# Mamba scan kernel: B rows and Gram sums moved to TensorE, bias operands folded into matmuls, split of quad 3 at 248

## What is computed

```python
# layer 0, per image, L = 4096 positions
u, z   = in_proj(group_norm(x))            # 96 -> 192 + 192 channels
u      = silu(causal_conv4(u) + conv_b)    # a bias per channel
dt, B, C = split(u @ x_proj.T, 6, 16, 16)
delta  = softplus(dt @ dt_proj.T + dt_bias)
h_t    = exp(delta_t * A) * h_(t-1) + delta_t * B_t * u_t   # 192 channels x 16 states
y      = (sum_n h_t[n] * C_t[n] + D * u) * silu(z)
x      = x + layernorm(y @ out_proj.T, eps=1e-5) * gamma + beta
# layer 1: t are tokens (4096 x 96)
t      = t + attention(layernorm(t, eps=1e-5))  # q (k' v): no softmax, so K'V folds into a 97 x 97 Gram matrix
t      = t + mlp(layernorm(t, eps=1e-5))        # 96 -> 384 -> 96, operands rounded to fp8, sums to fp16
```

## Time and profile before

| | |
|---|---|
| time of the runs | 2510.44 us median of 3 (2509.95 to 2512.78) |
| profiled execution, span from first to last instruction | 2508.8 us |
| busy share of the span | DVE 98%, POOL 96%, ACT 92%, PE 85% |
| mean granted clock of TensorE | 0.987 |

### The profile page before, as it was taken

The page is one execution under the profiler, slowest core; times in us unless marked ns, Lnnn a source line. Parts: engine busy times, 40 slices in busy tenths (PEclk is TensorE's granted clock), DMA queues, the critical chain, the costliest instruction groups (busy, mean ns, idle before and its releaser), DMA issues.

```text
span 2508.8 us, 35019 instructions
## 1 busy us (share of the span) xinstructions
PE 2142.1 (85%) x10314; PEld 826.0 (33%) x10314; DVE 2454.5 (98%) x2391; ACT 2314.7 (92%) x3960; POOL 2414.8 (96%) x655
## 2 busy tenths in 40 slices
PE   6788888888888888888888888888888888888878
PEld 3334434323323323323333323323323333333323
DVE  7999999999999999999999999999999999999986
ACT  5777777999999999999999999999999999999977
POOL 4999999999999999999999999999999999999991
PEclk8999999999999999999999999999999999999979
DMA  6555555556656656566566566566566565566542
GB/s 243 189 185 172 195 185 184 202 198 207 209 202 205 207 201 212 201 205 206 204 206 214 194 208 212 195 210 208 198 210 211 197 207 201 192 206 203 186 142 75
DMA packets 171388, 494.54 MB, mean 197 GB/s; under 512 B 23072, under 2 KB 44704, under 8 KB 154240
## 3 DMA queue, kind: packets, MB, share of 16 engines
q1 hardware_dynamic: 171200, 492.30, 57.9%
HBM read 400.33 MB, written 91.88 MB: 196 GB/s over the span
## 4 chain that ended last, share of the span: by engine, by line
POOL 40%; issue 40%; DVE 15%; PE 3%; ACT 1%; DMA 0%; POOLq 0%; DVEq 0%; SPq 0%; ACTq 0%
POOL R L676 20%; DVE R L1277 11%; POOL D L649 9%; POOL R L672 7%; POOL du L642 3%; DVE D L1261 2%; POOL D L658 2%; PE G L1568 1%; PE Y L1568 0%; DVE q L1357 0%; DVE dl L1287 0%; DVE G L1302 0%; DVE h L1471 0%; DVE h L1478 0%; PE Y L1645 0%
## 5 line engine op out<-in xcount | busy, mean ns | idle before, releaser
L1277 DVE TENSOR_TENSOR_SCAN R<-DA,R,D 128x512 f32<-128x512 f32 x1344 | 1630.2, 1263 | 1.0 <-ACT DA L840 1.0
L840 ACT ACTIVATE DA<-ds,kept_w 128x512 f32<-128x512 f32 x1536 | 1054.8, 688 | 139.9 <-DVE R L1277 127.1
L676 POOL TENSOR_TENSOR R<-R,Cs 128x2048 f32<-128x2048 f32 x255 | 970.9, 3819 | 4.0 <-DVE R L1277 2.6
L649 POOL TENSOR_TENSOR D<-us,Bs 128x2048 f32<-128x2048 f32 x193 | 736.9, 3818 | 8.8 <-DMA us<-lo_d 8.8
L672 POOL TENSOR_TENSOR R<-R,Cs 128x4096 f32<-128x4096 f32 x64 | 476.5, 7446 | 0.1
L1261 DVE TENSOR_TENSOR D<-us,PB 128x2048 f32<-128x2048 f32 x191 | 356.8, 1868 | 6.3 <-DMA us<-lo_d 6.3
L1645 PE MATMUL Y<-R,kept_w 128*32 128x512 f32 x2048 | 266.1, 615 | 13.9 <-POOL R L672 12.8
L1602 PE MATMUL G<-un,wcv 96*128 96x512 f32 x512 | 251.6, 614 | 29.5 <-ACT h L907 29.5
L1277 DVE TENSOR_TENSOR_SCAN R<-DA,D 128x512 f32<-128x512 f32 x192 | 221.7, 1204 | 2.1 <-ACT DA L840 2.1
L1605 PE MATMUL G<-un,wcv 96*64 96x256 f32 x1024 | 138.5, 392 | 60.1 <-ACT xq L888 58.9
L1568 PE MATMUL G<-st,kept_w 128*64 128x256 f32 (+1 forms) x384 | 108.9, 485 | 53.5 <-ACT st L802 53.5
(11 more groups left out here) (240 smaller groups left out, 3437.5 us busy)
## 6 DMA issues: line engine op xcount, KB each, us to landing
Bs<-bc_d SPq DMA_DIRECT2D x128, 512.0 KB, 5.6
us<-lo_d SPq DMA_DIRECT2D x64, 1024.0 KB, 6.3
ds<-lo_d SPq DMA_DIRECT2D x64, 1024.0 KB, 8.4
Cs<-bc_d SPq DMA_DIRECT2D x128, 512.0 KB, 4.7
us<-hi_d SPq DMA_DIRECT2D x64, 512.0 KB, 6.8
ds<-hi_d SPq DMA_DIRECT2D x64, 512.0 KB, 5.5
lo_d<-dl SPq DMA_DIRECT2D x64, 256.0 KB, 2.0
lo_d<-du SPq DMA_DIRECT2D x64, 256.0 KB, 2.0
```

Of the source, the lines that this page charges most:

```text
L649: nc.gpsimd.tensor_tensor(shaped(D[:, s % NDBU, :, :], s), low(us, s) if s in LOWS else high(us), of_states(Bs, s), ALU.mult).then_inc(don ...
L676: nc.gpsimd.tensor_tensor(shaped(R[:, s, :, 0:T], s), shaped(R[:, s, :, 1:S], s), of_states(Cs, s), ALU.mult).then_inc(hc_done.sem, 1)
L840: nc.scalar.activation(DA[j % NDA][:, :], ds[:, i, :], ACT.Exp, scale=A[:, j:j + 1]).then_inc(exp_done.sem, 1)
L1277: nc.vector.tensor_tensor_scan(R[:, s, q, 1:S], DA[j % NDA][:, :], D[:, s % NDBU, q, :], before, ALU.mult, ALU.add).then_inc(scanned.sem, 1)
```

## The change

Four parts, with the helper functions that carry them:

1. **Gram.** TensorE first multiplies G (SBUF) with an identity (`id97`) into G2, then adds the four token products; ScalarE copies the sum back to G (new `gram` on ScalarE, after decay(1, 2) and before `state_rows`). VectorE's add goes, save for the last two chunks.
2. **B rows.** `put_b` leaves ScalarE. TensorE makes PB from the state rows st with a selecting matrix of 32 rows (`bsel`): for quad 1 ahead of all else in an iteration, for quad 3 between `out_proj` and the centre matmuls, for the next chunk's quad 0 between `variance(g-1, 1)` and the conv. st gets two buffers.
3. **Biases.** A row of ones is added to un, sq, fsq and st, and conv_b, eps and dt_bias become a row of the weights; the activations lose their bias tensor. `state_rows` copies 64 rows in place of 128.
4. **Split.** `SPLIT = {3: 248}`: VectorE makes 16 columns more of each of the four blocks of quad 3, GpSimd 16 fewer.

```diff
-SPLIT = {3: 232}
+SPLIT = {3: 248}
...
+            sp_eng.dma_start(wcv[C:C + 1, 0, :], I["conv_b"]).then_inc(cb_in, 16)
...
-                    nc.scalar.activation(u[:, place(k) % 2, part(v)], src[v], ACT.Silu, bias=cb[:, v:v + 1])\
+                    nc.scalar.activation(u[:, place(k) % 2, part(v)], src[v], ACT.Silu)\
...
-                nc.scalar.activation(st[:, :], src[:, :], ACT.Identity, bias=one_row).then_inc(st_done.sem, 1)
+                nc.scalar.copy(st[0:64, k % 2, :], src[0:64, :]).then_inc(st_done.sem, 1)
...
-                nc.scalar.copy(PB[:, 0:n], Bs[:, h, w, 0:n]).then_inc(b_put.sem, steps_to(k, s))
...
-                nc.scalar.activation(rs[:, :], src[0:C, :], ACT.Ln, bias=epsn[0:C, :]).then_inc(post_ln.sem, 1)
+                nc.scalar.activation(rs[:, :], src[0:C, :], ACT.Ln).then_inc(post_ln.sem, 1)
...
+            def gram(k, src):
+                act.wait_ge(post_mm.sem, post_mm.at(k, 6))
+                if place(k) == 0 and there(k - CH):
+                    act.wait_ge(fold_mm.sem, fold_mm.at(k - CH, 1))
+                nc.scalar.copy(G[:, :], src[0:C + 1, 0:C + 1]).then_inc(gram_kept.sem, 1)
...
-                if there(g - 2):
-                    gram(g - 2, G2)
...
             def gram(k, o):
+                more = place(k) > 0 and k < LAST - 1
+                if more:
+                    pe.wait_ge(gram_kept.sem, gram_kept.at(k - 1))
+                    mm(o[0:C + 1, 0:C + 1], id97, G[:, :], start=True, stop=False)
...
+            def put_b(k, s):
+                if k == 0 and s == 1:
+                    return
+                if s == 3 and place(k + 3) == 0 and later(k + 3):
+                    pe.wait_ge(gn_act.sem, gn_act.at(k + 3, 4))
+                pe.wait_ge(st_done.sem, st_done.at(k))
+                pe.wait_ge(dbu_d.sem, dbu_d.at(k, BY_DVE[s] - steps_to(k, s)))
+                n = SPLIT.get(s, T)
+                one(PB[:, 0:n], bsel[:, BY_DVE[s] - 1, :], st[0:2 * STATE, k % 2, 0:n]).then_inc(b_put.sem, steps_to(k, s))
```

More of the change, by code:

```diff
@@ L777, in norm @@
                     act.wait_ge(front_mm.sem, front_mm.at(k - 1))
-                    nc.scalar.copy(un[:, 0:HALO], zero[0:C, 0:HALO])
-                nc.scalar.activation(un[:, lo:], un[:, lo:], ACT.Identity, bias=cgs[:, 1:2],
+                    nc.scalar.copy(un[0:C, 0:HALO], zero[0:C, 0:HALO])
+                nc.scalar.activation(un[0:C, lo:], un[0:C, lo:], ACT.Identity, bias=cgs[:, 1:2],
                                      scale=cgs[:, 0:1]).then_inc(normed.sem, 1)
@@ L871, in last_ln @@
                     act.wait_ge(post_dve.sem, post_dve.at(LAST - 1, 2))
-                nc.scalar.activation(rs[:, HALVES[h]], src[0:C, HALVES[h]], ACT.Ln, bias=epsn[0:C, :])\
+                nc.scalar.activation(rs[:, HALVES[h]], src[0:C, HALVES[h]], ACT.Ln)\
                     .then_inc(half_ln[h], 1)
@@ L897, in inv_ln_x2 @@
                 act.wait_ge(f_q8.sem, f_q8.at(m - 1))
-                nc.scalar.activation(frs[:, :], src[0:C, :], ACT.Ln, bias=epsn[0:C, :]).then_inc(f_ln.sem, 1)
+                nc.scalar.activation(frs[:, :], src[0:C, :], ACT.Ln).then_inc(f_ln.sem, 1)
             def inv_std_x2(m):
@@ L959, in iteration @@
                     decay(g, 1, 2)
+                if there(g - 2) and g - 2 < LAST - 1:
+                    gram(g - 2, G2)
                 if there(g + 1):
@@ L1087, in beginning @@
             def beginning():
-                nc.scalar.copy(un[:, 0:HALO], zero[0:C, 0:HALO])
+                nc.scalar.copy(un[0:C, 0:HALO], zero[0:C, 0:HALO])
                 act.wait_ge(x_in, 16)
                 act.wait_ge(gn_act.sem, gn_act.at(0))
-                nc.scalar.activation(un[:, HALO:], un[:, HALO:], ACT.Identity, bias=gsh[:, :],
+                nc.scalar.activation(un[0:C, HALO:], un[0:C, HALO:], ACT.Identity, bias=gsh[:, :],
                                      scale=gsc[:, :]).then_inc(normed.sem, 1)
@@ L1096, in beginning @@
                     act.wait_ge(front_mm.sem, front_mm.at(0, 1 + v))
-                    last = nc.scalar.activation(u[:, 0, part(v)], src[:, 0:T - H * v], ACT.Silu, bias=cb[:, v:v + 1])
+                    last = nc.scalar.activation(u[:, 0, part(v)], src[:, 0:T - H * v], ACT.Silu)
                     last.then_inc(silued.sem, 1)
@@ L1601, in conv @@
                     if v == 0:
[L1602 removed]
+                        last = mm(o[:, :], wcv[0:rows_of(t), t, 0:LOW], un[0:rows_of(t), t:t + T], start=(t == 0), stop=(t == TAPS - 1))
                         continue
                     for rows, cs in halves():
[L1605 removed]
+                        last = mm(o[rows, 0:H], wcv[0:rows_of(t), t, LOW:LOW + HIGH],
+                                  un[0:rows_of(t), t + cs.start:t + cs.stop],
                                   start=(t == 0), stop=(t == TAPS - 1))
@@ L1611, in z_proj @@
                 if v == 0:
-                    last = one(o[:, :], wz[:, 0:LOW], un[:, HALO:])
+                    last = one(o[:, :], wz[:, 0:LOW], un[0:C, HALO:])
                 else:
                     for rows, cs in halves():
-                        last = one(o[rows, to:to + H], wz[:, LOW:LOW + HIGH], un[:, HALO + cs.start:HALO + cs.stop])
+                        last = one(o[rows, to:to + H], wz[:, LOW:LOW + HIGH], un[0:C, HALO + cs.start:HALO + cs.stop])
                 last.then_inc(front_mm.sem, 1)
@@ L1630, in dt_proj @@
                 if v == 0:
-                    last = one(o[:, :], dtw[:, 0:LOW], st[:, :])
+                    last = one(o[:, :], dtw[0:65, 0:LOW], st[0:65, k % 2, :])
                 else:
                     for rows, cs in halves():
-                        last = one(o[rows, 0:H], dtw[:, LOW:LOW + HIGH], st[:, cs])
+                        last = one(o[rows, 0:H], dtw[0:65, LOW:LOW + HIGH], st[0:65, k % 2, cs])
                 last.then_inc(back_mm.sem, 1)
@@ L1714, in gram @@
                         pe.wait_ge(last_tokens, 1 + a // 2)
-                    last = mm(o[0:C + 1, 0:C + 1], tT[:, a, :], tT[:, a, :], start=(a == 0), stop=(a == T // 128 - 1))
+                    last = mm(o[0:C + 1, 0:C + 1], tT[:, a, :], tT[:, a, :], start=(a == 0 and not more),
+                              stop=(a == T // 128 - 1))
                 last.then_inc(post_mm.sem, 1)
+            def put_b(k, s):
[7 more added lines that the diff above has]
+                one(PB[:, 0:n], bsel[:, BY_DVE[s] - 1, :], st[0:2 * STATE, k % 2, 0:n]).then_inc(b_put.sem, steps_to(k, s))
             def fold(k, n, o):
@@ L1798, in iteration @@
                     pe.wait_ge(w_ready, 1)
+                if there(g):
+                    put_b(g, 1)
                 if there(g - 1):
@@ L2150 @@
         "skip": skip,
[L2151 removed]
+        "mask": (c[:, None] // hd == c[None, :] // hd) * hd ** -0.5,
     }
```

124 lines of the change are left out of this document (61 added, 63 removed).

## The result

The changed kernel takes 2533.55 us (median of 4 runs, 2531.08 to 2534.15), the kernel before 2510.39 beside it: a ratio of 1.0087, 95% interval 1.0073 to 1.0101. That is slower, as forecast, but by 23.2 us where 6.9 were forecast, and above the end of my range (2525). The profiled execution spans 2532.0 us against 2508.8, so it shows the whole difference: +23.15 us.

The account below looks back on a forecast made before the run. VectorE sets the pace, ScalarE and GpSimd close behind. First chunks of batches +3.0, plain chunks +4.9, first twelve chunks -1.0, the rest 0: +6.9 us on 2508.8, 2515.7, as a median 2517.3; range 2504 to 2525.

Parts of the forecast that it names:

- Steps 1 to 4: Plain chunk: state rows 0.39 us late behind Gram; TensorE 0.30 later; quad 3 adds 0.73; logarithm 0.36 later, `scale_out` 0.19.
- hole: TensorE's idle time ahead of `add_skip`: 1.18 us free, which the quad 1 matmul at 1.17 us just fits.
- The floor: Plain chunk: decay(2,1) ends later behind the state rows, so the scan needing it waits some 0.09 us.
- the 32-row tiles change nothing: Rival: no price for changing tile size, quad 3 matmul 0.42 us, plain chunks unchanged, 2510 to 2512 us; 25 in 100.
- the saving lands: Rival: neither floor nor `scale_out` is late, VectorE's saving gives -5 us or more, 2503 to 2505.5 us; 13 in 100.
- the plain chunk: 26 chunks without extra work in the whole pipeline: 0.19 us longer each through a later `scale_out`, 4.9 us together.
- the first chunk of a batch: Six chunks where VectorE already waited at `scale_out` and `variance` had no idle time ahead: 0.5 us longer each, 3.0 together.
- the 20 chunks taken as 0: Chunks with statistics, folds or set_batch: other work ahead of `scale_out` hides TensorE's delay; 0, between -0.1 and +0.19 us each.
- the whole -0.08: First 12 chunks: VectorE's net saving of 0.08 us a chunk (-0.15 for the add, +0.07 for the split) lands, -1.0 us.
- steps 1 to 3: State rows 0.39 us late behind Gram, TensorE 0.30 later, quad 3 matmul adding 0.73 ahead of the variance.
- the start: Before the first scan: one small DMA more on SP, taken as cancelling with shorter logarithms at the end, 0 us.
- The slack that the prediction worked out for `scale_out`: 0.40 us before `variance`, 0.19 before the logarithm, 0.09 of bias, 0.08 at `scale_out`: 0.76 in all.

Follow-up runs that it names:

- e1: The changed kernel with a 65-row selector for all three B-row matmuls, so their tile has the other matmuls' size: 2517.88 us, ratio 1.0021 to the kernel before.
- e2: The changed kernel with ScalarE's copy of G moved behind the state rows and decay(1,3): 2507.29 us, ratio 0.9977 to the kernel before.
- e9: The changed kernel with all three B rows back as ScalarE copies, Gram part, biases and split 248 kept: 2517.78 us, ratio 1.0024 to the kernel before.
- e7: The changed kernel with TensorE's quad 3 B-row matmul moved behind the two variances: 2863.05 us, ratio 1.1416 to the kernel before.
- e4: The changed kernel with the Gram part undone, VectorE adding to G again: 2514.19 us, ratio 1.0006 to the kernel before.
- e5: The changed kernel with the copy of G behind decay(1,3) and the quad 3 split back at 232: 2510.36 us, ratio 0.9996 to the kernel before.
- e6: The changed kernel with the copy of G behind decay(1,3) and the 65-row selector, split 248: 2504.61 us, ratio 0.9984 to the kernel before.
- e8: The changed kernel with Gram sum, B rows and split 232 put back, only the biases in matmul rows left: 2510.71 us, ratio 0.9998 to the kernel before.
- e10: The changed kernel with ScalarE's copy of G between the state rows and decay(1,3): 2507.71 us, ratio 0.9983 to the kernel before.
- e3: The changed kernel with quad 3's B row copied by ScalarE behind decay(2,1) instead of a TensorE matmul: 2526.66 us, ratio 1.0065 to the kernel before.
- e11: The changed kernel with copy of G behind decay(1,3), 65-row selector, and conv bias row's transfer behind the first weights': 2510.49 us, ratio 0.9992 to the kernel before.

## Why the prediction was wrong, by its own steps

**Right: what bounds the kernel, and the chain.** Steps 1 to 4 are in the rows almost as written. State rows +0.38 (forecast 0.39); TensorE +0.30 behind them (dt_proj at 11.45 instead of 11.16: 0.29); the quad 3 matmul 0.61 to the next start, 0.09 more at its entry and 0.08 on the matmul behind it, 0.78 (forecast 0.73); variance end +0.60 (0.55); logarithm +0.41 (0.36); `scale_out` +0.23 (0.19). The quad 1 matmul fits its hole: no wait appears at the gates that it could have held up in plain chunks. The floor, a scan waiting for decay(2,1), is there with 0.08 us (0.09), stays in e1 and goes when the copy moves. Of the rivals, "the 32-row tiles change nothing" is refuted by 0.36 us in e1, and "the saving lands" is true of e2, not of the change.

**Mis-sized: the plain chunk,** 0.25 for 0.19, 0.9 us over 26 chunks, and the first chunk of a batch, 0.53 for 0.5. The latter is near in part by luck: the forecast had all of it at `scale_out`, where VectorE waits for 0.31 us in chunk 16 (before 0.13), and missed 0.26 and 0.12 us of waits for decays ahead of two scans.

**Failed: the 20 chunks taken as 0.** This is the largest part of the miss, 8.15 of the 16.2 us between +6.9 and +23.1. The text said that with statistics, folds or set_batch an engine has work of its own ahead of `scale_out`, behind which TensorE's delay lies. It looked at one end of the chain, `scale_out`, and not at the new wait itself. In the statistics chunk the copy of G waits for a Gram group that stands behind the statistics' matmuls, and what it holds is not hidden: VectorE is later than before by 0.28 us at scan(1,3), 0.52 at scan(2,1), 0.68 at `scale_out`, 0.70 in the end. e9 (0.63 without any B row on TensorE) and e2 (-0.01 with the copy moved) show that nearly all of this is the copy's place. Over all 20 it was 8.15 us, of which 4.8 in the seven chunks of the statistics' place (4.5 in the six that have them), 1.9 in one second chunk (33) in which the clock fell for 3.4 us, and the rest mostly the plain chunk's 0.27 in the six second chunks.

**Failed: "the whole -0.08" in the first twelve,** -1.0, measured +4.7. 3.4 of this is chunk 1, where the clock was at its lower level for a stretch of 6.8 us that the execution of before did not have. Of the other kernels e7 had the same stretch (+3.1), e4, e5, e6, e8 and e10 had one of 3.4 us there (+1.0 to +1.8), and e1, e2, e3, e9 and e11 none (-0.4 to +1.05). That it makes the chunk longer is shown; that the change brings it on is not, since e2 and e10, which have the same matmuls, differ in it. What chunk 1 costs is the least sure part of the 23 us. Chunks 2 to 11 are +1.4 together. The prediction read from the earlier trace rows that of VectorE's own waits the one that recurs is `scale_out`'s. The same view of before has a larger one, for the second gate:

```profile
DVE yv L1298 <- PE Y L1649: 5.9, 9, 1.3
```

Eight of these nine waits lie in the first twelve chunks (0.31 to 0.46 us each in chunks 3 to 8). In the changed kernel they are gone in chunks 3 to 8, and waits at `scale_out` stand in their place, 0.27 us in chunks 2 to 7 and 0.55 in chunk 8, with 0.65 us ahead of scan(1,3) in the statistics chunk 5. With either cost of the chain away the same ten chunks come to -0.7 (e1) and -1.3 (e2), near what the prediction took. So steps 1 to 3 reach VectorE in them too, which the text had ruled out, since `spin` stands there in place of the centre matmuls.

**Open: the start,** +0.97 where 0 was taken; see e11.

**What the sum left out.** The prediction added terms along one chain with slack. The plain chunk is a table of the two costs, as the difference from before:

| | small tile for quad 3 | full tile |
|---|---|---|
| copy of G ahead of the state rows | +0.25 | +0.02 |
| copy of G behind decay(1,3) | -0.10 | -0.10 |

Either cost taken away frees VectorE almost wholly or wholly; both together give nothing more in this chunk. Removing the copy's place is worth 0.35 with the small tile and 0.12 with the full one; that 0.12 is the floor at scan(2,1) and little else. The slack that the prediction worked out for `scale_out` (0.76 us) fits: the change delays TensorE's matmuls up to the variance by 0.29 + 0.78 = 1.07 us, e1 by 0.29 + 0.42 = 0.71, e2 by 0.78 - 0.09 (its state rows end earlier) = 0.69, and only the first exceeds it. But the text did not ask what the order of one queue alone was worth. The e2 order could have been read from the rows: a copy that nobody needs until the next Gram sum stood ahead of state rows on which TensorE was already waiting.
